# Single rows of the edge gathers, addressed by bytes and shared between SyncE and ScalarE

## What is computed

```python
# layer 0: mean over in-edges of h[src], then a dense map
neighbor_sum = segment_sum(h[src], dst)
# layer 1: gated difference
theta = h[dst] - h[src]
w = sigmoid(relu(theta @ W1 + b1) @ W2 + b2)
agg = segment_sum(w * theta, dst)
# layer 2: mean over in-edges of relu(h @ Wp.T + bp)[src], elu, norm
# layer 3: one of eight maps by edge type, weighted
msg = all_h[etypes, src] * norm          # all_h: 8 maps of h
h_out = segment_sum(msg, dst) + h @ loop_weight
```

## Time and profile before

| | |
|---|---|
| median of three runs | 5199.56 us |
| profiled execution | 5203.18 us |
| its span | 5200.9 us |
| GpSimd busy | 3626.3 us, 70% |
| TensorE busy | 3831.0 us, 74% |
| VectorE busy | 2942.5 us, 57% |
| ScalarE busy | 1574.2 us, 30% |

### The profile page before, as it was taken

The page is one execution under the profiler, slowest core; times in us unless marked ns, Lnnn a source line. Parts: engine busy times, 40 slices in busy tenths (PEclk is TensorE's granted clock), DMA queues, the critical chain, the costliest instruction groups (busy, mean ns, idle before and its releaser), DMA issues.

```text
span 5200.9 us, 90088 instructions
## 1 busy us (share of the span) xinstructions
PE 3831.0 (74%) x22383; PEld 2948.3 (57%) x22393; DVE 2942.5 (57%) x9882; ACT 1574.2 (30%) x5791; POOL 3626.3 (70%) x3862
## 2 busy tenths in 40 slices
PE   3889999665565565666566488879899999999544
PEld 2345555555555555555556455545677777777543
DVE  7998876565556566666666744444544444332332
ACT  5555544433333333333343401133112222221000
POOL 5355553577777777777777477757777777777776
PEclk7799999788778778778877799989999999998655
DMA  4234444555555555555555565556222222222222
GB/s 125 71 124 131 144 146 140 156 165 160 159 163 161 162 160 164 161 162 164 161 164 163 155 200 192 197 179 244 61 53 53 53 53 53 53 52 54 55 74 55
DMA packets 319322, 668.55 MB, mean 129 GB/s; under 512 B 77939, under 2 KB 169762, under 8 KB 309330
## 3 DMA queue, kind: packets, MB, share of 16 engines
q0 software_dynamic: 153664, 365.93, 26.2%
q1 hardware_dynamic: 163122, 295.92, 17.1%
q10 hardware_dynamic: 2016, 0.92, 0.1%
HBM read 545.42 MB, written 113.38 MB: 127 GB/s over the span
## 4 chain that ended last, share of the span: by engine, by line
POOL 44%; PE 25%; issue 16%; DVE 9%; DMA 2%; ACT 2%; DVEq 1%; SPq 1%; ACTq 0%; POOLq 0%
POOL rows L1611 36%; POOL third L1611 8%; PE ps L2801 6%; PE ps L2696 4%; PE ps L2708 4%; PE ps L2786 3%; PE ps L2759 3%; DVE tmp L2095 2%; PE ps L2766 1%; PE ps L2645 1%; DVE oneh L2004 1%; DVE turned_words L2096 1%; DVE rows L2096 1%; ACT h L1786 1%; DMA rows<-tab_h,idx_src 1%
## 5 line engine op out<-in xcount | busy, mean ns | idle before, releaser
L1611 POOL DMA_INDIRECT rows<-tab_rel,third x1185 | 1170.9, 988 | 361.3 <-issue 355.5
L1611 POOL DMA_INDIRECT rows<-tab_hp,idx_src x1107 | 1065.8, 963 | 341.2 <-issue 334.7
L1611 POOL DMA_INDIRECT rows<-tab_h,idx_src x790 | 772.4, 978 | 540.5 <-PE ps L2766 274.8
L2824 PE MATMUL ps<-third 128*128 128x128 f32 x3126 | 594.8, 350 | 711.7 <-DVE third L2125 711.2
L2824 PEld LDWEIGHTS ps<-third 128*128 128x128 f32 x3126 | 512.5, 249 | 781.7 <-DVE third L2125 781.2
L1834 ACT ACTIVATE turned_words<-turned_words 128x128 f32<-128x128 f32 x1563 | 463.0, 297 | 1227.5 <-DVE turned_words L2140 1218.0
L2801 PE MATMUL ps<-third,h 128*128 128x385 bf16 (+1 forms) x3626 | 744.4, 336 | 44.0 <-DMA h<-cnt_d 23.9
L2759 PE MATMUL ps<-oneh,rows 128*128 128x128 f32 x2406 | 400.1, 319 | 243.0 <-DMA rows<-tab_rel,third 140.6
L2759 PEld LDWEIGHTS ps<-oneh,rows 128*128 128x128 f32 x2406 | 351.3, 224 | 306.5 <-issue 163.2
L2801 PEld LDWEIGHTS ps<-third,h 128*128 128x128 bf16 x3626 | 352.0, 100 | 294.2 <-issue 31.8
L1611 POOL DMA_INDIRECT third<-tab_hp,idx_src x437 | 421.2, 964 | 133.2 <-issue 131.7
(11 more groups left out here) (305 smaller groups left out, 5687.9 us busy)
## 6 DMA issues: line engine op xcount, KB each, us to landing
third<-dst_flat SPq DMA_DIRECT2D x390, 256.0 KB
cnt_d<-h SPq DMA_DIRECT2D x37, 1568.0 KB, 5.8
h<-cnt_d SPq DMA_DIRECT2D x37, 1568.0 KB, 7.2
third<-tab_hp SPq DMA_DIRECT2D x2432, 1.0 KB
key<-tab_rel SPq DMA_DIRECT2D x2304, 0.5 KB
tab_rel<-third SPq DMA_DIRECT2D x49, 512.0 KB, 3.3
rows<-tab_rel,third POOLq DMA_INDIRECT x1185
rows<-tab_hp,idx_src POOLq DMA_INDIRECT x1107
```

Source lines behind the costliest of these rows:

```text
L1611: pool.indirect_dma_start(out=to[:, t, 0:n], out_offset=None, in_=table[:, :], in_offset=bass.IndirectOffsetOnAxis(ap=idx[:, col:col + 1], ...
L2824: last = pe.matmul(ps_t[sl][:, t * P:(t + 1) * P], onehT[:, sl, t * P:(t + 1) * P], pwin[:, st["v"] % 2, :], start=True, stop=True)
```

## The change

- The lists get longer: in layer 1 SyncE every 13th group from 14, ScalarE every 33rd from 39; in layer 3 SyncE every 11th from 90 + 14, ScalarE every 33rd from 90 + 42. Each entry now names how many rows go out per turn (12 for SyncE, 4 for ScalarE) and how many turns before the group's turn the copy stands (0 for SyncE, 2 and 4 for ScalarE).
- VectorE multiplies the row numbers by the size of a row, by a shift, once per layer, in the entry `single_offsets` of turn 1. SyncE and ScalarE wait for it where they begin a tile; SyncE's waits for the index rows in `edges_begin` go.
- The rows are addressed in a flat view of the table in bytes; the registers are loaded by another call, which loads 12 (or 4) values without a bounds check at run time.
- ScalarE waits for the tables at the start of the edge stages.
- The index rows to load become 40 (from 19) in layer 1 and 34 (from 18) in layer 3.

```diff
-SINGLES = {1: (("sp", 20, 20),), 3: (("sp", 18, 16),)}
-ROW_LOAD = 8
+SINGLES = {1: (("sp", 14, 13, 12, 0), ("act", 39, 33, 4, 2)), 3: (("sp", 14, 11, 12, 0), ("act", 42, 33, 4, 4))}
...
-            for who, first, step in SINGLES.get(layer, ()):
-                singles[who] = list(range(g0 + first, ng - ROW_LOAD, step))
+            for who, first, step, load, lead in SINGLES.get(layer, ()):
+                singles[who] = list(range(g0 + first, ng - 8, step))
+                pace[who] = load, lead
                 single_of.update((g, (who, j)) for j, g in enumerate(singles[who]))
 
             def single_rows(g):
                 for who in singles:
+                    load, lead = pace[who]
                     for j, at in enumerate(singles[who]):
-                        r0 = (g - (at - P // ROW_LOAD - 1)) * ROW_LOAD
+                        r0 = (g - (at - lead + (-P // load) - 1)) * load
...
+                        if lead and g == at - lead:
+                            single_copy(at)
...
-                if g in single_of:
-                    who, j = single_of[g]
-                    n_moved[g] = s_moved[layer, who][j % 2], s_moved[layer, who][j % 2].up(16)
...
+                if g in single_of and g not in n_moved:
+                    single_copy(g)
...
-                single_rows(g0 + turn)
+                if layer in SINGLES:
+                    single_rows(g0 + turn)
+                    if turn == 1:
+                        plan.append(("single_offsets", dict(layer=layer, at=s_rowoff.up())))
...
-                    sp.wait_ge(s_rowidx.handle, 16 * len(single_groups[1]))
...
-                    sp.wait_ge(s_rowidx.handle, n_rowidx)
...
-                    sp.load(row_regs, idx_single[layer][at:at + 1, r0:r0 + ROW_LOAD])
-                    for r in range(ROW_LOAD):
-                        row = sp.snap(row_regs[r], min_val=0, max_val=table.shape[0] - 1)
-                        sp.dma_start(to[r0 + r:r0 + r + 1, :], table[bass.ds(row, 1), :]).then_inc(full.handle, 16)
+                    if st["offsets"]:
+                        sp.wait_ge(s_rowoff.handle, st["offsets"])
+                    size = 4 * table.shape[1]
+                    flat = table.bitcast(mybir.dt.uint8).rearrange("r b -> (r b)")
+                    _, begins = nc.values_load_multi_w_load_instructions(
+                        idx_single[layer][at:at + 1, r0:st["r1"]], engines=[sp.engine], min_val=0, max_val=(table.shape[0] - 1) * size,
+                        skip_runtime_bounds_check_because="a row's number times its size, with numbers as the gathers use them")
+                    for r, begin in enumerate(begins):
+                        sp.dma_start(to[r0 + r:r0 + r + 1, :].bitcast(mybir.dt.uint8),
+                                     flat[bass.ds(begin, size)].rearrange("(o b) -> o b", o=1)).then_inc(full.handle, 16)
...
                 elif kind == "edges_begin":
+                    if st["layer"] in SINGLES:
+                        for k in range(3):
+                            if st["tab"][k]:
+                                act.wait_ge(s_tab[k].handle, st["tab"][k])
                     act.wait_ge(s_mm.handle, st["mm"])
...
+                elif kind == "single_offsets":
+                    layer = st["layer"]
+                    n = len(single_groups[layer])
+                    dve.wait_ge(s_rowidx.handle, 16 * sum(len(single_groups[k]) for k in SINGLES if k <= layer))
+                    shift = (4 * tables[layer][0].shape[1]).bit_length() - 1
+                    v = idx_single[layer][0:n, :].bitcast(U32)
+                    dve.tensor_scalar(v, v, shift, None, ALU.logical_shift_left).then_inc(s_rowoff.handle, 1)
```

More of the change, by code:

```diff
@@ L869, in single_rows, with single_copy @@
                 for who in singles:
+                    load, lead = pace[who]
                     for j, at in enumerate(singles[who]):
-                        r0 = (g - (at - P // ROW_LOAD - 1)) * ROW_LOAD
+                        r0 = (g - (at - lead + (-P // load) - 1)) * load
                         if 0 <= r0 < P:
+                            free = None
                             if r0 == 0:
+                                assert s_rowoff.value
                                 single_full[who, j] = s_single[layer, who][j % 2].up(16 * P)
-                            free = n_moved[singles[who][j - 2]] if j > 1 and r0 == 0 else None
-                            plan.append(("single_rows", dict(layer=layer, who=who, j=j, r0=r0, free=free)))
+                                free = n_moved[singles[who][j - 2]] if j > 1 else None
+                            plan.append(("single_rows", dict(layer=layer, who=who, j=j, r0=r0, r1=min(P, r0 + load), free=free,
+                                                             offsets=s_rowoff.value if r0 == 0 else 0)))
+                        if lead and g == at - lead:
+                            single_copy(at)
+            def single_copy(g):
+                who, j = single_of[g]
+                n_moved[g] = s_moved[layer, who][j % 2], s_moved[layer, who][j % 2].up(16)
+                plan.append(("single_copy", dict(layer=layer, who=who, j=j, slot=g % slots, t=tiles[g] - 1, free=slot_free.get(g % slots),
+                                                 full=single_full[who, j])))
             def gather(g):
@@ L1402, in gnn_program @@
             single_groups[layer] = []
-            for who, first, step in SINGLES[layer]:
+            for who, first, step, *_ in SINGLES[layer]:
                 row_at_single[layer, who] = len(single_groups[layer])
-                single_groups[layer] += range((0, 0, 0, HEAD_END)[layer] + first, ng - ROW_LOAD, step)
-        n_rowidx = 16 * sum(len(groups) for groups in single_groups.values())
+                single_groups[layer] += range((0, 0, 0, HEAD_END)[layer] + first, ng - 8, step)
         def sync_program(sp):
-            row_regs = [sp.alloc_register(f"row{k}") for k in range(ROW_LOAD)]
             sp.wait_ge(s_pad.handle, n_pad)
@@ L1792, in scalar_program @@
                     act.copy(wsum[0:width, 0:P + 1], ps[st["bank"]][0:width, 2 * P:3 * P + 1]).then_inc(s_wlo.handle, 1)
+                elif kind == "single_rows" and st["who"] == "act":
+                    layer, j, r0 = st["layer"], st["j"], st["r0"]
+                    table, full = tables[layer][0], s_single[layer, st["who"]][j % 2]
+                    to = single_at[layer, st["who"]][j % 2]
+                    if st["free"]:
+                        act.wait_ge(st["free"][0].handle, st["free"][1])
+                    at = row_at_single[layer, st["who"]] + j
+                    if st["offsets"]:
+                        act.wait_ge(s_rowoff.handle, st["offsets"])
+                    size = 4 * table.shape[1]
+                    flat = table.bitcast(mybir.dt.uint8).rearrange("r b -> (r b)")
+                    _, begins = nc.values_load_multi_w_load_instructions(
+                        idx_single[layer][at:at + 1, r0:st["r1"]], engines=[act.engine], min_val=0, max_val=(table.shape[0] - 1) * size,
+                        skip_runtime_bounds_check_because="a row's number times its size, with numbers as the gathers use them")
+                    for r, begin in enumerate(begins):
+                        act.dma_start(to[r0 + r:r0 + r + 1, :].bitcast(mybir.dt.uint8),
+                                     flat[bass.ds(begin, size)].rearrange("(o b) -> o b", o=1)).then_inc(full.handle, 16)
+                elif kind == "single_copy" and st["who"] == "act":
+                    layer, j, sl = st["layer"], st["j"], st["slot"]
+                    act.wait_ge(s_single[layer, st["who"]][j % 2].handle, st["full"])
+                    if st["free"]:
+                        act.wait_ge(st["free"][0].handle, st["free"][1])
+                    act.dma_start((rows_hp if layer == 1 else rows_at)[sl][:, st["t"], 0:tables[layer][0].shape[1]],
+                                 single_at[layer, st["who"]][j % 2]).then_inc(s_moved[layer, st["who"]][j % 2].handle, 16)
                 elif kind == "evict3":
```

13 lines of the change are left out of this document (7 added, 6 removed).

## The result

The changed kernel takes 5173.42 us (median of six, 5169.32 to 5180.35) against 5199.63 us (six, 5193.86 to 5201.55): ratio 0.995, 95% interval 0.994 to 0.996. It is 0.5% faster; the forecast was 5165 us and 0.7%. The medians lie 26 us apart, while single executions of the change spread over 11 us.

The account below looks back on a forecast made before the run. GpSimd's single-row gathers were taken to bound the edge stages of layers 1 and 3. Profiled 5203.2 - 45 (tiles) + 7 (index rows) + 3 (lag) = 5168, less 3.6 for the median: 5165 us, range 5148 to 5280.

Parts of the forecast that it names:

- GpSimd's beat and the tiles taken off it: Edge stages of layers 1 and 3: a gather starts every 1.25 us; 20 and 16 fewer save 45 us.
- The 3 us of the sum: End of the program: late tiles in layer 3 leave TensorE a lag to catch up, priced at 3 us.
- Row cost 0.336: SyncE's single rows: byte offsets remove the multiplication, so a row takes 0.336 us instead of 0.42.
- The upper bound 0.42: SyncE's row cost if the address still needs a register operation: 0.42 us per row.
- Load of 12: SyncE's register load: 0.79 us plus four registers at 35 ns each, 0.93 us; bounds 0.79 and 1.19.
- The third rival: SyncE's loads grow with their registers, 1.19 instead of 0.93 us: 5195 us; chance 0.07.
- SyncE in layer 1: SyncE's rows, loads and rest take 1844 us against GpSimd's 1935, so they fit with 90 us to spare.
- Layer 3: SyncE needs 1436 us and has 1436, no room left; tiles late by under some 40 us stop only TensorE.
- ScalarE at nothing: ScalarE's four rows per turn, 1.9 to 2.1 us, fit into its waits in layers 1 and 3; taken as 0.
- The second rival: ScalarE holds up TensorE in layer 3, deciding from 0.25 us per turn; 5274 us at 1 us; chance 0.09.
- Index rows: Queue ahead of tab_pb's stores before layer 3: 16 more index rows cost 7 us, between 3 and 10.
- The sum: Whole kernel: profiled 5203.2 - 45 + 7 + 3 = 5168; the median lies 3.6 us lower, 5165 us, 0.7% faster.

Follow-up runs that it names:

- experiment 1: Changed kernel with word instead of byte offsets, so one multiplication per row again: 5631.36 us against 5197.86 of the kernel before, ratio 1.0831.
- experiment 3: Changed kernel with layer 3's 34 index rows fetched behind the stores of tab_pb: ratios 1.0199, 1.0168, 1.0212 to the kernel before, on chips where that takes 6316 to 6402 us.
- experiment 4: Changed kernel without ScalarE's tiles, SyncE alone fetching 55: 6441.29 against 6401.65 us of the kernel before (ratio 1.0056) and 6355.54 against 6319.22 (1.0047).
- experiment 6: Byte addresses alone, with the kernel before's 37 tiles on SyncE, loads of 8, no ScalarE: ratios 0.9658, 0.9638, 0.9638 to the kernel before, on chips where that takes 6316 to 6402 us.

## Why the prediction was right

- **GpSimd's beat and the tiles taken off it**: 20 x 1.25 forecast, 24.0 us measured in layer 1; 17.0 for 20 - 3 in layer 3. The mean per gather over heads and edges of layer 3 is 1.2925 us for 1.290. The 3 us of the sum were priced for a lag at the end of the program, and that lag did not come: the tail after the last gather is 11.8 us as before. What takes their place is gathers of 991 ns instead of 988, 3.5 us over 1169 of them, so this term was hit by luck.
- **Row cost 0.336**: 335.6 ns measured, a mean of a usual 322 ns and one row in sixty over 450 ns. Part of the fit is luck: inside a turn the median row took 419 ns before and takes 322 now, so the multiplication was worth 97 ns and not 84, and the rare long rows bring the mean back to the forecast. The upper bound 0.42 was nearly tested by experiment 1, with 0.41.
- **Load of 12**: 969 ns median, 1.00 us to the next instruction. The sum had 0.93 in layer 1 and 0.98 in layer 3, so that is 22 + 7 = about 30 us more. The term was mis-sized because four more registers cost 232 ns and not 140 (35 each had been taken from other engines' loads). The third rival (1.19) is ruled out. So is the rule of the Trainium skill's page Runtime: NRT & Kernel Launch, section Instruction fetch mechanics, for these loads: 12 registers in 0.97 us are 81 ns each, not 200.
- **SyncE in layer 1**: 1844 us of work were forecast with 90 of room; 79 us of waits were left. **Layer 3**: 1436 forecast, 1435.8 measured without waits. The forecast let SyncE begin 15 us after GpSimd's first gather of the edges (3680 against 3665); it began 23.2 us after it (3669.74 against 3646.50). So there was somewhat less than the "no room" of the sum, and the forecast held because TensorE's 33.4 us of waiting fell within the slots.
- **ScalarE at nothing**: its waits for TensorE's products before evictions in layer 3 stayed (380.3 us for 392.0), and TensorE's wait for ScalarE's eviction is 22.7 us (PE L2760 <- ACT acc), 22.3 before. The second rival did not occur on this chip.
- **Index rows**: +8.8 for 7, within 3 to 10. GpSimd's wait for the last store itself is 40.6 us, where 37 was named, for 30.07 before. The term had counted that part of the queue is hidden by h; experiments 3, 4 and 6 show on their chips that it is the 18 rows of before that are hidden, and that further ones are not.
- **The sum**: 35 us forecast for the span, 28.8 measured. The 6.2 us between them are 3.5 ahead of layer 1, 1.8 of index rows and 1.0 of layer 1's gathers. What failed in size is thus mainly the start, for which I had written 0 (the 21 more index rows of layer 1 and ScalarE's waits there stand behind it in the program); its cause is open, and the differences are hardly above the scatter. The median missed by more, 8.4 us: the forecast took off 3.6 us, by which the profiled execution of before lay above its median, and that of the change lies only 0.6 above.
- **What the prediction missed**: every bound was set from the rows of one chip. SyncE's row period is the number on which the change stands, and it is half as long again on three other chips (514 ns in experiment 3). The range of 5148 to 5280 can hold only for the chips on which the kernel before takes 5200 us.

## What to carry to other kernels

Work may be moved to a queue only as far as that queue's own time per item, times the items, stays under the pace of the engine relieved; a register operation of 33 ns on each item decided here between 0.5% faster and 8% slower. Ahead of a store that waits for data, a queue has free places up to the moment when the data are there (18 index rows here), and each one beyond costs most of its own time (0.55 of 0.64 us). Leave such a queue room for other chips: where it was the bound, making items cheaper helped (experiment 6), and filling the saved time with more items took the gain back (experiment 4).

## What the runs showed that was not expected

- One kernel, 5198 to 5200 us in two comparisons and 6316 to 6402 us on three other chips: there SyncE's MOVE, 29 ns otherwise, took over 100 ns in 1001 to 1169 cases per run (about 0.5 us each). It is not SyncE alone: GpSimd has its own unexplained waits there, and layer 2, which has no single rows, takes 583 to 591 us for 498.
- The number of these long MOVEs hardly depends on the number of rows: 1019 with 4736 rows (experiment 6, second run), 1061 with 7040 (experiment 4, second run).
- A register load from on-chip memory costs SyncE 734 ns for 8 registers and 969 for 12, ScalarE 495 for 4: 59 ns per register between 8 and 12 on SyncE, where 35 were taken from the other engines' rows.
- An ALU_OP of 33 ns lengthens a row by 70 ns, so that the gap around an instruction costs as much as the instruction.
